# Layer norm of a fused two-layer kernel: centring and scaling on ScalarE instead of VectorE, and the first tile's loads and stores on two queues

## The reference

```python
q, k, v = silu(x @ Wq), silu(x @ Wk), silu(x @ Wv)
log_f = log_sigmoid(x @ Wf1 @ Wf2); beta = sigmoid(x @ Wbeta) * 2
k = l2norm(k)
# for each token: two rank-one updates of S, then o = q . S
y = out * sigmoid(x @ Wog1 @ Wog2), normed for each head, @ Wo
# experts: 64 of width 64, 8 chosen for each token by a router, and a shared one
y += cw[e] * (silu(x @ We_gate[e]) * (x @ We_up[e])) @ We_down[e]
```

## Time and profile before

| | us |
|---|---|
| median of 3 runs | 2104.19 (2104.09 to 2106.93) |
| the profiled execution, its own time | 2104.4 |
| span of the profiled execution | 2102.7 |
| mean granted TensorE clock | 0.895 |

### The profile page before, as it was taken

How to read it: one execution, slowest core, us unless ns; L and a number is a source line. 1 busy time by engine, 2 the same in 40 slices (tenths; PEclk the granted TensorE clock), 3 DMA queues, 4 the chain that set the end, 5 groups by cost and what they waited for, 6 DMA issues and landing times. The chain is left out here.

```text
span 2102.7 us, 32686 instructions
## 1 busy us (share of the span) xinstructions
PE 1635.4 (78%) x8418; PEld 1185.5 (56%) x8418; DVE 1603.5 (76%) x4329; ACT 1137.1 (54%) x1811; POOL 1018.5 (48%) x1108
## 2 busy tenths in 40 slices
PE   3286787886868768778787399898999997888886
PEld 2164454554545436445454298787988875555554
DVE  3499999999999999999999535444344457777774
ACT  1365464564645646546454154444555447777774
POOL 2577778686787877887887400000000002332332
PEclk9598898897978988989898599999999999999998
DMA  5420020110200202002001411001110010000000
GB/s 83 108 56 1 1 66 1 25 43 1 66 0 4 63 2 51 15 0 61 1 11 38 103 21 26 19 14 27 21 26 11 11 31 9 15 22 15 22 15 13
DMA packets 140707, 58.82 MB, mean 28 GB/s; under 512 B 94743, under 2 KB 135180, under 8 KB 140556
## 3 DMA queue, kind: packets, MB, share of 16 engines
q1 hardware_dynamic: 140556, 57.19, 12.1%
HBM read 36.05 MB, written 21.10 MB: 27 GB/s over the span
## 5 line engine op out<-in xcount | busy, mean ns | idle before, releaser
L612 ACT ACTIVATE shared_rings<-pb 128x512 f32<-128x512 f32 (+1 forms) x784 | 434.7, 598 | 360.6 <-PE pb L639 318.4
L688 PE MATMUL pb<-hid,shared_down 128*128 128x512 f32 x528 | 308.0, 669 | 159.7 <-POOL hid L490 157.1
L486 POOL TENSOR_TENSOR hid<-shared_rings 128x512 f32<-128x512 f32 x256 | 333.9, 1304 | 178.6 <-ACT shared_rings L612 164.2
L490 POOL TENSOR_TENSOR hid<-hid,shared_rings 128x512 f32<-128x512 f32 x256 | 329.6, 1288 | 20.6 <-POOL hid L486 1.0
L1818 DVE SCALAR_TENSOR_TENSOR l_acc<-l_pb,l_gtok,l_acc 128x128 f32<-128x128 f32 x512 | 144.3, 344 | 256.1 <-PE l_pb L1462 256.1
L637 PE MATMUL pb<-xt_hi,shared_hi 128*128 128x512 f32 (+1 forms) x264 | 192.3, 729 | 101.6 <-ACT shared_rings L612 101.6
L1373 ACT ACTIVATE l_hid<-l_pb,l_cols 128x512 f32<-128x512 f32 x256 | 169.3, 688 | 182.8 <-PE l_pb L1462 182.5
L1462 PEld LDWEIGHTS l_pb<-l_big,l_hid 128*128 128x128 f32 x2048 | 247.1, 192 | 10.6
L1462 PE MATMUL l_pb<-l_big,l_hid 128*128 128x128 f32 x2048 | 247.9, 275 | 0.0
L1287 POOL TENSOR_TENSOR l_ql<-l_rope,l_qh 128x512 f32 x8 | 10.3, 1286 | 459.4 <-ACT l_qh L1367 459.4
L688 PEld LDWEIGHTS pb<-hid,shared_down 128*128 128x128 f32 x528 | 101.1, 207 | 217.0 <-POOL hid L490 191.3
(11 more groups left out here) (319 smaller groups left out, 3803.7 us busy)
## 6 DMA issues: line engine op xcount, KB each, us to landing
z_scratch<-zs SPq DMA_DIRECT2D x128, 81.0 KB, 3.0
zr<-z_scratch SPq DMA_DIRECT2D x8, 1296.0 KB, 8.0
x_sb<-in_L_attn_x_dram SPq DMA_DIRECT2D x32, 64.0 KB, 2.0
shared_rings<-in_L_ffn_We_gate_dram SPq DMA_DIRECT2D x4, 512.0 KB, 5.8
shared_rings<-in_L_ffn_We_up_dram SPq DMA_DIRECT2D x4, 512.0 KB, 6.9
g_scratch<-zs SPq DMA_DIRECT2D x8, 256.0 KB, 2.8
y_scratch<-yo SPq DMA_DIRECT2D x8, 256.0 KB, 2.1
shared_down<-in_L_ffn_W_dram SPq DMA_DIRECT2D x4, 512.0 KB, 5.6
```

What stands on the lines that cost most here:

```text
L486: pool.tensor_tensor(hid1[:, :], g, u, ALU.mult).then_inc(s_h1, 1)
L490: pool.tensor_tensor(hid[:, (p + par) % 2, :], hid1[:, :], c, ALU.mult).then_inc(s_h, 1)
L612: act.activation(dst, pb[0:n, what, :], ACT.Silu if what == 0 else ACT.Copy).then_inc(s_ev, 1)
L688: last = pe.matmul(pb[:, SUM, :], wd[0:n, p, :], hid[0:n, (p + par) % 2, :], start=(p == 0), stop=(p == PAIRS), skip_group_check=True)
```

## The change

Three things. (1) In every tile the mean's subtraction and the scaling by the inverse deviation leave VectorE. VectorE only makes the negative mean (128 x 4, at the same place) and the reciprocal; ScalarE centres with four activations (`centre`, at slot 9, followed at once by the square that stood at slot 12) and scales with four (`scaled`, at slot 16), each with a column of `stat` as bias or scale. (2) The first loads go out on two queues: SP issues x, the identity and the factor weights, then the chunks; ScalarE issues the four head weights and then the gate weights, one-hot, bias and triangle. (3) The work ahead of tile 0 is in another order: layer norm first, then the weights' split; the router's products go behind all projections into a bank of their own; ScalarE stores the last quarter of z (4 of 16 pieces), and SP the rest; the selectors (`sel`) are made after the layer norm. The diff, cut to its core (a line with # names the engine):

```diff
-        stat = sb("stat", [P, 2, NS])
+        stat = sb("stat", [P, 4, NS])
...
-        LN, PREP, POST, ROUTE = 2, 7, 4, 57
+        LN, PREP, POST, ROUTE = 3, 7, 4, 57
...
-        LN_AT, ROUTE_AT = {(0, 0): 0, (1, 0): 1, (3, 0): 2, (4, 0): 3, (4, 1): 4, (6, 1): 5}, 11
+        LN_AT, ROUTE_AT = {(0, 0): 0, (1, 0): 1, (3, 0): 2, (4, 0): 3, (6, 1): 5}, 11
+        CENTRE_SLOT, SCALE_SLOT = 9, 16
...
-        SMALL = 13
+        SMALL, HEADS, LATE = 5, 4, 4
...
# SyncE: onehot, tri, bias64, gate_w, Wq, Wk, Wv and wbeta leave its queue; then pass_z
+                    if alone and s == NS - 1:
+                        continue
...
-            pass_z(0, 0, False)
+            pass_z(0, 0, False, True)
...
# ScalarE
+            for at, name in ((ZQ, "L0_attn_Wq"), (ZK, "L0_attn_Wk"), (ZV, "L0_attn_Wv")):
+                act.dma_start(wp[:, :, at:at + HD0], d[name].rearrange("i (h c) -> i h c", h=H0)).then_inc(s_heads, 16)
+            act.dma_start(wbeta[:, :], d["L0_attn_Wbeta"]).then_inc(s_heads, 16)
+            act.dma_start(gate_w[:, :], d["L0_ffn_gate_w"]).then_inc(s_late, 16)
...
+            def factors():
+                act.wait_ge(s_w1t_ps, 1)
+                act.activation(wf1T[:, :, :], pb[0:HD0, 0, 0:2 * P].rearrange("p (a b) -> p a b", a=2), ACT.Copy).then_inc(s_w1t, 1)
...
+            def head_weights():
+                act.wait_ge(s_heads, HEADS * 16)
+                act.activation(wp[:, :, ZB], wbeta[:, :], ACT.Copy).then_inc(s_w12, 1)
+                act.wait_ge(s_w12_ps, 1)
...
+            def centre(t):
+                act.wait_ge(s_ln, t * LN + 2)
+                for s in range(NS):
+                    last = act.activation(xc[:, s, :], x_sb[:, s, :], ACT.Identity, bias=stat[:, 2, s:s + 1])
+                last.then_inc(s_xc, 1)
                 act.wait_ge(s_xc, t + 1)
                 act.activation(xn[:, :, :], xc[:, :, :], ACT.Square).then_inc(s_sq, 1)
+            def scaled(t):
+                act.wait_ge(s_ln, t * LN + 3)
+                for s in range(NS):
+                    last = act.activation(xn[:, s, :], xc[:, s, :], ACT.Copy, scale=stat[:, 3, s:s + 1])
+                last.then_inc(s_xn, 1)
+            def norm(t, alone):
+                if alone:
+                    factors()
                 act.wait_ge(s_var, t + 1)
...
+                    if ahead and r == CENTRE_SLOT:
+                        centre(t + 1)
+                    if ahead and r == SCALE_SLOT:
+                        scaled(t + 1)
...
-            norm(0)
+            act.wait_ge(s_eps, 2)
+            centre(0)
+            norm(0, True)
+            scaled(0)
+            head_weights()
             for k in range(-1, UNITS):
-                project(0, 0, k, k % 4)
+                project(0, 0, k, k % 4, True)
+            act.wait_ge(s_zc, UNITS)
+            for b in range(BS):
+                act.dma_start(z_dram[0, NS - 1, b].rearrange("h n c -> n h c"),
+                              zs[TP * b:TP * (b + 1), NS - 1, :].rearrange("p (h c) -> p h c", h=H0)).then_inc(s_zst, 16)
+            act.wait_ge(s_lg, 1)
+            router_scores(pb[:, SUM, :])
...
# TensorE
+            pe.wait_ge(s_late, LATE * 16)
+            pe.transpose(pb[:, 1, 0:E0], gate_w[:, :], ident[0:E0, 0:E0]).then_inc(s_w1t_ps, 1)
...
             for k in range(-1, UNITS):
+                if k == 0:
+                    pe.wait_ge(s_wp, 4)
...
+            router(0, pb[:, SUM, :], True).then_inc(s_lg, 1)
...
# VectorE: layer_norm
                 elif stage == 1:
                     dve.wait_ge(s_ln, t * LN + 1)
-                    dve.scalar_tensor_tensor(out=xc[:, :, :], in0=over(x_sum, D), scalar=-1.0 / D, in1=x_sb[:, :, :],
-                                             op0=ALU.mult, op1=ALU.add).then_inc(s_xc, 1)
+                    dve.tensor_scalar(stat[:, 2, :], x_sum, -1.0 / D, None, ALU.mult).then_inc(s_ln, 1)
...
-                    dve.reciprocal(x_rstd, stat[:, 1, :]).then_inc(s_ln, 1)
-                elif stage == 4:
-                    dve.wait_ge(s_ln, t * LN + 2)
-                    dve.tensor_tensor(xn[:, :, :], xc[:, :, :], over(x_rstd, D), ALU.mult).then_inc(s_xn, 1)
+                    dve.reciprocal(stat[:, 3, :], stat[:, 1, :]).then_inc(s_ln, 1)
...
-            for stage in range(6):
+            for stage in range(4):
                 layer_norm(0, 0, stage)
+            head_weights()
+            layer_norm(0, 0, 5)
+            dve.wait_ge(s_late, LATE * 16)
+            dve.tensor_copy(sel[:, :, :], over(onehot[:, :], F0)).then_inc(s_sel, 1)
+            dve.wait_ge(s_s0, 1)
```

More of the change, by code:

```diff
@@ L180, in layer0 @@
         other, penalty = (spare[:, NS * G0 * i:NS * G0 * (i + 1)].rearrange("p (s g) -> p s g", s=NS) for i in range(2))
[L181 removed]
+        x_sum, cw_sum = (spare[:, 2 * NS * G0 + NS * i:2 * NS * G0 + NS * (i + 1)] for i in range(2))
         s_x = sem("x_loaded")
[L185 removed]
+        s_small = sem("factor_weights_loaded")
+        s_heads = sem("head_weights_loaded")
+        s_late = sem("router_constants_loaded")
         s_stage = [sem(f"stage_loaded{i}") for i in range(3)]
@@ L311, in _, with pass_z @@
                 load_chunk(k)
-            def pass_z(t, par, later):
+            def pass_z(t, par, later, alone=False):
                 for s in range(NS):
@@ L514, in _ @@
         def _(act):
[L515 to L524, removed]
@@ new lines, in _ @@
+            act.dma_start(tri[:, :], d["c_tri"].rearrange("(o c) -> o c", o=1).to_broadcast([P, G0 * G0])).then_inc(s_late, 16)
+            def factors():
[5 more added lines that the diff above has]
+                act.wait_ge(s_w12_ps, 1)
+                for a, at in ((0, ZF), (1, ZG)):
+                    act.activation(wp[:, :, at:at + HD0], pb[:, 2, D * a:D * (a + 1)].rearrange("p (h c) -> p h c", h=H0),
+                                   ACT.Copy).then_inc(s_w12, 1)
@@ L530, in norm, with router_scores, project @@
+            def norm(t, alone):
+                if alone:
+                    factors()
                 act.wait_ge(s_var, t + 1)
                 act.activation(stat[:, 1, :], stat[:, 0, :], ACT.Sqrt, bias=eps[:, 0:1], scale=1.0 / D).then_inc(s_std, 1)
-            def project(t, par, k, side):
+            def router_scores(bank):
+                act.activation(scores, bank[:, 256:512].rearrange("p (s e) -> p s e", s=NS), ACT.Sigmoid).then_inc(s_sc, 1)
+            def project(t, par, k, side, alone=False):
@@ L545, in project @@
                     act.activation(zs[:, 3, WIDE:ZW], bank[:, 0:REST], ACT.Copy).then_inc(s_zc, 1)
-                    act.activation(scores, bank[:, 256:512].rearrange("p (s e) -> p s e", s=NS), ACT.Sigmoid).then_inc(s_sc, 1)
+                    if not alone:
+                        router_scores(bank)
                 else:
@@ L642, in _ @@
             for a in range(2):
-                pe.transpose(pb[0:HD0, 0, P * a:P * (a + 1)], wf1[:, a, :], ident[:, :])
-            last = pe.transpose(pb[:, 1, 0:E0], gate_w[:, :], ident[0:E0, 0:E0])
+                last = pe.transpose(pb[0:HD0, 0, P * a:P * (a + 1)], wf1[:, a, :], ident[:, :])
             last.then_inc(s_w1t_ps, 1)
@@ L649, in _, with project @@
             last.then_inc(s_w12_ps, 1)
-            pe.wait_ge(s_wp, 4)
-            def project(t, par, k, side):
+            pe.wait_ge(s_late, LATE * 16)
+            pe.transpose(pb[:, 1, 0:E0], gate_w[:, :], ident[0:E0, 0:E0]).then_inc(s_w1t_ps, 1)
+            def project(t, par, k, side, alone=False):
                 bank = pb[:, side, :]
@@ L668, in project @@
                 elif k == 1:
-                    split3(bank[:, 0:REST], hi[:, sub[3]], lo[:, sub[3]], wp_hi[:, WIDE:ZW], wp_lo[:, WIDE:ZW])
-                    for s in range(NS):
-                        last = split3(bank[:, 256 + E0 * s:256 + E0 * (s + 1)], hi[:, sub[s]], lo[:, sub[s]], wr_hi[:, :], wr_lo[:, :], first=False)
+                    last = split3(bank[:, 0:REST], hi[:, sub[3]], lo[:, sub[3]], wp_hi[:, WIDE:ZW], wp_lo[:, WIDE:ZW])
+                    if not alone:
+                        last = router(par, bank, False)
                 else:
@@ L675, in project, with router @@
                 last.then_inc(s_zp, 1)
+            def router(par, bank, first):
+                for s in range(NS):
+                    sub = slice(P * s, P * (s + 1))
+                    last = split3(bank[:, 256 + E0 * s:256 + E0 * (s + 1)], xt_hi[par][:, sub], xt_lo[par][:, sub], wr_hi[:, :], wr_lo[:, :], first=first and s == 0)
+                return last
             def router_weights(t):
```

36 lines of the change are left out of this document (14 added, 22 removed).

## The result

| | before | after |
|---|---|---|
| median, us | 2105.56 (2104.09 to 2107.07, 4 runs) | 2085.18 (2082.90 to 2086.40, 4 runs) |
| span of the profiled execution, us | 2102.7 | 2084.4 |
| mean granted TensorE clock | 0.895 | 0.895 |

The ratio is 0.9902, with a 95% interval of 0.9885 to 0.9919: 20.6 us less, between 17.1 and 24.2. Forecast were 2086 us and 17.8 less. The time came out near the forecast, but in part by luck: the start gave 3 us less than its terms, and a like amount comes from something that no term held, the place of buffers in memory.

The account below looks back on a forecast made before the run. Neither side was taken as free: VectorE and the experts' group (PE, ScalarE, GpSimd) hold the chain by turns. Start 13.9, tile 0 0.96 and tiles 1 to 6 2.9 sum to 17.8 us less: 2086, range 2080 to 2093.

Parts of the forecast that it names:

- Start to the projection, 8.8 us: Ahead of tile 0: ScalarE free at 6.9 us, then a 10.5 us chain; first projection at 17.4, 8.8 us earlier.
- Z's way, 5.1 us: Tile 0, projection to load of zr: stores begin 3.0 us sooner, issue saves 2.1; together 5.1, bounds 3.0 and 7.7.
- 2.1 saved, if ScalarE's four run beside them: Tile 0's z stores: SP issues 12 of 16 at 0.52 us each, saving 2.1 us if ScalarE's four run alongside.
- The bound of 3.0: Lower bound of the gain between tile 0's projection and load of zr: 3.0 us if the DMA engines set the pace.
- From zr to the recurrence, unchanged: Start, after zr: everything unchanged; later routing hidden in VectorE's 16.5 us idle, about 4 left; second x's wait about 20.
- The whole start: Everything ahead of tile 0's recurrence: 8.8 us to the projection plus 5.1 on z's way, 13.9 us less.
- rival C: Start: DMA engines hold the z stores and ACT queue's loads land later; gain 10.8 us, total 2089.5; chance 20%.
- VectorE's 0.96 us a tile: Steady tiles, steps 1 and 4: VectorE loses two 512-element operations worth 0.48 us each, 0.96 a tile.
- How much of it arrives, 3.8 us: Of VectorE's saving, 0.96 us arrives in tile 0 and 0.48 in each of tiles 1 to 6; 3.8 in all.
- Rival A: Steady tiles: all of VectorE's 0.96 us arrives in each tile; 2083.5, about 2079 with the start's upper bound; chance 15%.
- ScalarE's work hidden: Slots 9 and 16: ScalarE's added activations fit its idle time, cost 0 on the path; wait before L531 stays above zero.
- my 1.15: ScalarE's four activations with a pointer, for centring or scaling, priced at 1.15 us: 0.37 each, 0.26 apart.

Follow-up runs that it names:

- The last experiment: Kernel after plus three edits: gate's store ahead of z stores, all z stores on SyncE's queue, small ScalarE copy for an earlier table load; 2074.36 us, ratio 0.9873.
- norm alone: Kernel before with only the layer norm's centring and scaling of tiles 1 to 7 moved to ScalarE, old start; 2089.58 us, ratio 0.9952.
- z on one queue: Kernel after with all 16 z stores of tile 0 issued by SyncE, none by ScalarE; 2077.77 us, ratio 0.9896.
- wide `stat`: Kernel before with only `stat` enlarged from 2 to 4 rows, no instruction changed; 2094.62 us, ratio 0.9978.
- pad: Kernel before with an unused 32-byte buffer declared ahead of `hid1`; 2095.89 us, ratio 0.9981.
- start alone: Kernel after with its new start, but the old layer norm on VectorE in tiles 1 to 7; 2081.70 us, ratio 0.9911.
- before twice: Kernel before and its unchanged repetition with a second profile; the repetition took 2102.03 us, its neighbours a median of 2099.35.
- the narrow one: Old buffer placement; its 944.2 is kernel after with `stat` at its old size and the new rows behind all other buffers: 2083.80 us, ratio 0.9922.

## Why the prediction was right, point by point

- **Start to the projection, 8.8 us:** measured 8.2 (17.99, forecast 17.4). The closeness is in part luck, for two steps were wrong and nearly cancel. ScalarE's first activation began at 8.65, where the sum had it at 6.9: its table load came behind its wait, 1.75 us late. VectorE's casts took 2.66 us (14.51 to 17.17) instead of 3.85, 1.19 less; the forecast had named up to 1.8 for this overlap with GpSimd. The last experiment shows that the table's lateness cost nothing in the end: the cast ends behind GpSimd's subtraction whenever it starts. The chain that the sum added up as far as the first cast was thus not the one that set the projection; that was the landing of the first chunk of expert weights and GpSimd's split of it.
- **Z's way, 5.1 us: the mis-sized term.** It measured 2.8 (from the projection to the load of zr 21.75 before, 18.97 after). Its first piece, the stores 3.0 us earlier behind the projection, is there to the tenth (7.83 to 4.84). The second, "2.1 saved, if ScalarE's four run beside them", measured -0.2 against before, and over all kernels nothing: 12.8 to 14.2 us with two queues, 12.6 to 13.9 with one. The bound of 3.0, "if the DMA engines set the pace", was the case, and the earlier trace rows said so: share 1.35 at 120 GB/s. I had set the pace of SyncE's issue against it at the wrong place: what counts is when the last store has landed, and in after that was 36.88, 7.15 us behind the end of SyncE's last issue (29.73) and 0.08 ahead of the load of zr (before: 47.94, 5.55 behind 42.39). The Trainium skill (DMA: Bandwidth & Descriptors, Issuing engines are not separate DMA queues) has it that a second issuing engine saves only the initiation; the traces agree. With two queues the last issue of after ended at 29.73 instead of 31.20 us, and the last store landed no earlier (36.88 against 35.91).
- **From zr to the recurrence, unchanged:** 24.96 us before, 25.08 after. VectorE's idle time ahead of its first product fell from 16.48 to 9.80, not to about 4, and the router's later place was hidden. The second x was waited for 19.5 us (19.8 before). The whole start is 10.9 instead of 13.9, in this pair and on the mean of all kernels. That is rival C's 10.8, by its mechanism in part: the DMA engines held the stores, but no load came late.
- **VectorE's 0.96 us a tile:** exact, 0.47 or 0.48 at steps 1 and 4.
- **How much of it arrives, 3.8 us:** not contradicted, and not shown. The two stages "tiles" with the new norm against the old, at like placement: 941.7 (after, norm alone, z on one queue) against 944.3 (wide `stat`, pad, start alone), 2.6 less; and 944.2 against 948.7 (before twice) at the narrow one, 4.5 less. Executions of like kernels lie up to 6 apart. The waits at step 13 of the tiles 1 to 6 point the forecast's way: they sum to 6.9 us on the mean in the first three kernels and 3.6 in the other three, 0.55 a tile more, where 0.5 was forecast. But of the first three the kernel after alone has 11.4; the other two have 4.3 and 5.0. The scaling back on VectorE moved the time by less than its uncertainty. Rival A is the less likely, and it is not excluded. What the forecast's reading missed is why VectorE waited at step 13: the store of the gate, in the middle of the stretch that it gave to ScalarE and the experts. With that store moved the wait is gone from both kernels.
- **ScalarE's work hidden:** yes. Its wait for VectorE before L554 stayed above 1.8 us. Three times ScalarE stood up to 2.1 us at slot 9 for VectorE's small instruction, where the text expected it in tile 0 alone; VectorE's next need was late enough. The Trainium skill's price for four activations with a pointer (ScalarE: Activation LUTs, What ACT_TABLE_LOAD costs), an estimated 1.27 us, was nearer to the 1.28 measured than my 1.15. Its rule to keep such work on VectorE is not borne out here, where ScalarE had idle time: the kernels with the work on ScalarE are no slower.
- **What no term held: placement.** That `stat` grew by 32 bytes is worth 4.0 to 4.6 us on the kernel before (by the two ratios), and likely as much here, where it was not shown. It made up for the start's missing three, and that is luck: without it an estimated 2089 would have been measured, inside the range, but rival C's time and not the forecast's.

## What to carry to other kernels

A wait that returns in every tile names the engine that signals, not the cause: follow the signaller's own waits back first. Here it ended at a store that SyncE issued four pieces too late, worth 7.6 us in one kernel and 11.8 in the other, more than the layer norm's move was forecast to bring. Spreading the z stores over two queues brought nothing, because they landed long behind their issue; read when the last one lands, and the DMA share in between, before counting issue time as a gain. And compare such a stretch over several kernels: a single pair was 1.4 us apart by scatter. And when a change alters the size of a buffer, compare the mean durations of untouched instructions before giving its gain to the code.

## What the runs showed of the hardware

- GpSimd's product of 128x512 f32 took 1304 to 1307 ns with the buffers from `hid1` on in their old place, and 1281 to 1284 ns with them 32 bytes further, over 256 of them some 6 us of GpSimd. Which operand's address does it was not tried.
- ScalarE's first table load was not issued ahead of the wait in front of the first activation (7.35 us, although ScalarE's queue was free at about 6.2); with an activation in front whose wait was long over it began at 5.94.
- A cast of VectorE from and to SBUF (128x648) stood still while GpSimd's subtraction of 128x1024 ran: it took 0.97 to 2.12 us in eight kernels, by how early it began, and ended 0.34 to 0.36 us behind the subtraction in all of them. The 0.85 us of before is no undisturbed time either: there, and in the five others with the old start, it ended 0.35 us behind GpSimd's first split instruction. The Trainium skill (SBUF — State Buffer, SBUF: two separate sides) describes this as a lock of a shared port pair that one of the two engines holds for its whole instruction; these rows agree with it.
- In after the z stores ran at 163 to 166 GB/s at a DMA share of 0.82 to 0.94 and then at 97 to 102 GB/s at a share of 1.35 to 1.37, until 34 us; with one queue at 155 to 163 and then 129 at 1.27.
